# A decoder kernel on one core: attention normalised in channel layout, with its denominators taken from ScalarE's accumulators

## What is computed

```
qh = (q @ Wq + bq).reshape(b, s, H, HD).transpose(0, 2, 1, 3)
kh = (k @ Wk + bk).reshape(b, s, H, HD).transpose(0, 2, 1, 3)
vh = (v @ Wv + bv).reshape(b, s, H, HD).transpose(0, 2, 1, 3)
scores = jnp.einsum('bhqd,bhkd->bhqk', qh, kh) * HD ** (-0.5)
scores = jnp.where(causal, -jnp.inf, scores)
attn = jax.nn.softmax(scores, axis=-1)
out = jnp.einsum('bhqk,bhkd->bhqd', attn, vh)
out = out.transpose(0, 2, 1, 3).reshape(b, s, DIM)
return out @ Wo + bo
```

## Time and profile before

| | |
|---|---|
| median of 3 runs | 371.97 us (371.9 to 372.0) |
| the profiled execution | 369.38 us, its span 367.60 us |
| TensorE matmuls busy | 338.3 us (92% of the span) |
| TensorE weight loads busy | 280.1 us (76%) |
| VectorE busy | 254.6 us (69%) |
| ScalarE busy | 238.9 us (65%) |
| GpSimd busy | 163.5 us (44%) |
| granted TensorE clock | 1.00 throughout |

### The profile page before, as it was taken

How to read it: one execution, slowest core, us unless ns; L and a number is a source line. 1 busy time by engine, 2 the same in 40 slices (tenths; PEclk the granted TensorE clock), 3 DMA queues, 4 the chain that set the end, 5 groups by cost and what they waited for, 6 DMA issues and landing times.

```text
span 367.6 us, 8998 instructions
## 1 busy us (share of the span) xinstructions
PE 338.3 (92%) x3283; PEld 280.1 (76%) x3299; DVE 254.6 (69%) x555; ACT 238.9 (65%) x586; POOL 163.5 (44%) x148
## 2 busy tenths in 40 slices
PE   7878679999999999999999999999999998989697
PEld 3657457987789877987789867987789866858596
DVE  5674786677766976677775976678765966482974
ACT  4552663776756866677847766677848764787551
POOL 4237150364615366363625457362634550445340
PEclk9999999999999999999999999999999999999999
DMA  5940102022031400413023400404014300013300
GB/s 151 307 172 1 31 2 107 37 62 85 1 112 78 144 0 17 171 33 110 0 66 120 143 0 14 169 7 137 0 47 141 116 6 10 30 16 116 116 29 30
DMA packets 22314, 26.97 MB, mean 73 GB/s; under 512 B 2896, under 2 KB 20112, under 8 KB 22288
## 3 DMA queue, kind: packets, MB, share of 16 engines
q1 hardware_dynamic: 21472, 26.52, 22.3%
q10 hardware_dynamic: 816, 0.10, 0.2%
HBM read 24.51 MB, written 2.10 MB: 72 GB/s over the span
## 4 chain that ended last, share of the span: by engine, by line
PE 77%; DVE 9%; issue 7%; ACT 4%; POOL 1%; DMA 1%; ACTq 0%; DVEq 0%; POOLq 0%
PE c L1208 22%; PE a L1208 16%; PE b L1208 14%; PE b1k L1344 7%; PE b1k L1208 6%; PE b2k L1208 4%; DVE negmax L912 2%; PE c L1371 2%; ACT prob L596 1%; ACT probT L558 1%; PE a L1223 1%; DVE scD L893 1%; PE b2k L1223 1%; DMA wk_c<-in_L_attn_Wk 1%; PE a L1301 1%
## 5 line engine op out<-in xcount | busy, mean ns | idle before, releaser
L460 POOL TENSOR_TENSOR w_lo<-w_in,w_hi 128x512 fp32r<-128x512 f32 x32 | 40.8, 1305 | 30.4 <-ACT w_hi L558 26.3
L596 ACT ACTIVATE prob<-b,negmax 128x128 f32<-128x128 f32 x124 | 36.1, 398 | 25.4 <-DVE negmax L912 25.4
L1344 PE MATMUL b1k<-ident,prob 128*128 128x128 f32 x256 | 40.0, 279 | 9.3 <-ACT probT L558 4.5
L466 POOL TENSOR_TENSOR w_lo<-w_in,w_hi 128x512 fp32r<-128x512 f32 x28 | 35.5, 1287 | 28.6 <-ACT w_hi L558 26.8
L453 POOL TENSOR_TENSOR rstA<-varA,minus_half 128x16 f32<-128x16 f32 x8 | 23.4, 2927 | 49.2 <-DVE varA L1047 49.2
L1344 PEld LDWEIGHTS b1k<-ident,prob 128*128 128x128 f32 x256 | 28.1, 140 | 17.3 <-ACT prob L596 7.2
L558 ACT ACTIVATE w_hi<-w_in 128x512 fp32r<-128x512 f32 x64 | 39.1, 653 | 2.6 <-PE b L1208 2.6
L1208 PE MATMUL c<-xTC_hi,w_hi 128*128 128x256 f32 x108 | 31.8, 294 | 0.8 <-DVE xTC_lo L862 0.8
L919 DVE COPY probT<-b1k 128x512 f32<-128x512 f32 x32 | 22.0, 687 | 13.1 <-PE b1k L1344 13.0
L1208 PE MATMUL c<-w_hi,h_hi 128*128 128x256 f32 x96 | 30.8, 321 | 0.1
L1208 PE MATMUL c<-xTC_lo,w_hi 128*128 128x256 f32 x108 | 30.5, 282 | 0.0
(11 more groups left out here) (301 smaller groups left out, 1110.4 us busy)
## 6 DMA issues: line engine op xcount, KB each, us to landing
w_in<-in_L_ffn_w SPq DMA_DIRECT2D x16, 1024.0 KB, 5.6
x_in<-in_x SPq DMA_DIRECT2D x8, 256.0 KB, 2.8
c_in<-in_ctx SPq DMA_DIRECT2D x8, 256.0 KB, 2.9
out<-x2b SPq DMA_DIRECT2D x7, 256.0 KB, 2.2
b_cur<-in_L_ffn_b SPq DMA_DIRECT2D x8, 128.0 KB, 3.0
W_sb<-in_L_attn_W SPq DMA_DIRECT2D x2, 256.0 KB, 4.2
decay_sb<-in_decay SPq DMA_DIRECT2D x1, 512.0 KB, 3.8
h_in<-in_L_xattn_Wk SPq DMA_DIRECT2D x1, 256.0 KB, 4.3
```

The lines of the kernel that those rows point to most:

```text
L460: pool.tensor_tensor(w1_lo[:, :, part], w1_in[:, :, part], w1_hi[:, :, part].bitcast(F32), ALU.subtract).then_inc(s_w1lo, 1)
L466: pool.tensor_tensor(w2_lo[:, part, :], w2_in[:, part, :], w2_hi[:, part, :].bitcast(F32), ALU.subtract).then_inc(s_w2lo, 1)
L596: ins = nc.scalar.activation(prob[:, u % PR, g, :], score_banks[u][:, g * P:(g + 1) * P], ACT.Exp, bias=negmax[:, u, g:g + 1], scale=-1.0)
L1344: ins = nc.tensor.transpose(b1k[:, g * P:(g + 1) * P], prob[:, u % PR, g, :], ident[:, :])
```

## The change

The attention is no longer brought back to tokens to be normalised.

- `exps` gives each ACTIVATE an accumulator output: den[:, u, g] is the row sum of the exponentials, the denominator for each token and head. At blocks 0 and 4 it waits for the reciprocals of the step before (`s_rden`).
- v_pad loses its ones. A head's values stand in the first or the second 16 of its 32 columns, the rest is zero, and `with_values` accumulates two blocks into the same 32 rows. So both sequences fit into one bank (c0, in step 8 a0), and that bank is in channel order of the output as Wo is now loaded: its rows are permuted by eight loads of 16 partitions where there were four of 32 (`WO_LOADS`).
- VectorE's `denominators` takes the reciprocals of den and copies each 16 times side by side (rtok); TensorE's `reciprocals` transposes rtok in four pieces, ScalarE copies them to rdT.
- VectorE's `normalise_attention` multiplies the bank with rdT (attT), ScalarE's `attention_out` rounds it to attT_hi, VectorE's `split_attention` makes attT_lo.
- `pv_out`, `values_to_tokens`, `divide` and `attention_transposes` go. `values` adds the bias in two instructions instead of one, and GpSimd clears all of v_pad at the start.

```diff
-WO_LOADS = 4
+WO_LOADS = 8
...
-        PV_BANK = [c0, b3]
+        PV_BANK = c0
...
-        PV_LAST = [a0, b3]
+        PV_LAST = a0
...
-            for j in range(4):
-                sp.dma_start(xw_in[XG * j:XG * (j + 1), 3, :, :], xWo_v[j % 2, j // 2]).then_inc(s_inO, 16)
+            for j in range(WO_LOADS):
+                sp.dma_start(xw_in[XD * j:XD * (j + 1), 3, :, :], xWo_v[j // 4, j // 2 % 2, j % 2]).then_inc(s_inO, 16)
...
+                    if u % PR == 0 and later(b):
+                        act.wait_ge(s_rden, 2 * b - 1 + u // PR)
                     for g in range(G):
                         ins = nc.scalar.activation(prob[:, u % PR, g, :], score_banks[u][:, g * P:(g + 1) * P],
-                                                   ACT.Exp, bias=negmax[:, u, g:g + 1], scale=-1.0)
+                                                   ACT.Exp, bias=negmax[:, u, g:g + 1], scale=-1.0,
+                                                   accum_out=den[:, u, g:g + 1])
...
-                def pv_out(seq):
-                    act.wait_ge(s_pv, 8 * b + 4 * seq + 4)
...
-                    copy(pvT[:, :], pv_banks[seq][:, :], s_pvT)
...
+                def reciprocals(bank):
+                    act.wait_ge(s_rT, b + 1)
+                    if later(b):
+                        act.wait_ge(s_aT, b)
+                    copy(rdT[:, :, :], bank[:, :].rearrange("p (c t) -> p c t", c=C), s_rdT)
+
+                def attention_out():
                     act.wait_ge(s_aT, b + 1)
-                    copy(attT_hi[:, :, :], bank[:, :].rearrange("p (c t) -> p c t", c=C), s_attT)
+                    if later(b):
+                        act.wait_ge(s_yB, b)
+                    copy(attT_hi[:, :, :], attT[:, :, :], s_attT)
...
+                def denominators(seq):
+
+                    dve.wait_ge(s_prob, 8 * b + PR * (seq + 1))
                     if later(b):
-                        dve.wait_ge(s_aT, b)
-                    kv = k_bank[:, :].rearrange("p (h e) -> p h e", e=VP)
-                    nc.vector.reciprocal(rden[:, seq, :], kv[:, :, XD]).then_inc(s_rden, 1)
+                        dve.wait_ge(s_rT, b)
+                    nc.vector.reciprocal(rden[:, seq, :], den[:, PR * seq:PR * (seq + 1), :]
+                                         .rearrange("p r g -> p (r g)")).then_inc(s_rden, 1)
                     dve.wait_ge(s_rden, 2 * b + seq + 1)
...
+                    nc.vector.tensor_copy(rtok[:, seq, :, :].rearrange("p c (g r e) -> p c g r e", g=G, r=2),
+                                          of_head.unsqueeze(4).broadcast_to([P, C, G, 2, XD])).then_inc(s_rexp, 1)
+
+                def normalise_attention():
+                    dve.wait_ge(s_pv, 8 * (b + 1))
+                    dve.wait_ge(s_rdT, b + 1)
...
+                    nc.vector.tensor_tensor(attT[:, :, :], pv_bank[:, :].rearrange("p (c t) -> p c t", c=C),
+                                            rdT[:, :, :], ALU.mult).then_inc(s_aT, 1)
...
+                def split_attention():
+                    dve.wait_ge(s_attT, b + 1)
+                    nc.vector.tensor_tensor(attT_lo[:, :, :], attT[:, :, :], attT_hi[:, :, :].bitcast(F32),
+                                            ALU.subtract).then_inc(s_attTlo, 1)
...
+                    col = r // 2 * T + bk * P
                     for h in range(G):
                         head = XH // C * (h // 2) + 2 * r + h % 2
-                        ins = mm(bank[VP * h:VP * (h + 1), r * P:(r + 1) * P], v_pad[:, bk, head, :],
-                                 probT[:, u % PR, h, :])
+                        ins = mm(bank[VP * h:VP * (h + 1), col:col + P], v_pad[:, bk, head, :], probT[:, u % PR, h, :],
+                                 start=(r % 2 == 0), stop=(r % 2 == 1))
...
-                def values_to_tokens(seq):
...
-                def attention_transposes(bank):
...
+                def reciprocals(bank):
+                    pe.wait_ge(s_rexp, 2 * (b + 1))
+                    transposes(bank, rtok[:, :, :, :].rearrange("p b c n -> p b (c n)"), s_rT)
```

137 lines of the change are left out of this document (56 added, 81 removed).

## The result

| | before | after |
|---|---|---|
| median of 4 runs | 371.94 us (371.62 to 372.0) | 384.14 us (382.69 to 384.56) |
| the profiled execution | 369.38 us, span 367.6 | 384.56 us, span 382.7 |
| granted TensorE clock, mean of the span | 1.000 | 0.982 |
| a regular step (mean of steps 2 to 6) | 41.76 us | 43.40 us |

The changed kernel is slower by 3.5% (ratio 1.0347, 95% interval 1.0311 to 1.0382). The forecast was 384.7.

The account below looks back on a forecast made before the run. TensorE was taken as the bound on average, with ScalarE setting its pace in two stretches. The terms summed to 208d - 8.15, +12.6 us at d = 0.1, giving 384.7 us against a median of 371.97; range 368 to 400.

Parts of the forecast that it names:

- The price d: ScalarE's extra cost of one accumulating exponential beyond a plain one, taken as 0.1 us, with 256 such exponentials in all.
- the free sums: Rival: the accumulator leaves beside the output, d between 0 and 0.03, total 363.8 (370 at 0.03); chance 0.16.
- the full readout: Rival: each sum costs d = 0.2 like a lone 128x1 instruction, total 405.5; chance 0.18.
- 28 x 0.092 - 0.88: Regular step, forecast as 28d - 0.88 us more each, over five steps 140d - 4.4; here with the measured d.
- 16d: Regular step, first exponentials to second scores: four blocks in ScalarE's gapless piece add +16d.
- 12d - 0.88: Regular step from the second scores on: +4d, then +8d - 0.48, then -0.40 up to the projection.
- -8.15: Whole program: the part of the forecast sum without d, chiefly from removed transposes, copies and waits, in us.
- 208d: Whole program: the readouts that lengthen the run, 208 of 256, each costing d.
- the rival on the other side: The free sums: only the transposes count, so the kernel gets faster, 363.8 us; chance 0.16.
- 24d - 1.3: Step 1: six blocks' readouts count, less 0.47 of ScalarE idle time, 0.44 and 0.40.
- 20d - 0.55: Step 7: readouts add 16d + 4d; fewer transposes and waits, less one more VectorE pair, give -0.55.
- 24d - 1.9: Step 8: readouts add 8d and 16d - 0.5; removed transposes and waits give -0.3 and -1.1.

Follow-up runs that it names:

- e2: The changed kernel without accumulator outputs, den set once to a constant 64 so denominators are not computed; 375.57 us, ratio 1.0120.
- e6: e5 without accumulator outputs, denominators again a constant 64; 367.45 us, ratio 0.9905.
- e1: The kernel before, with only an accumulator output that nobody reads added to every exponential; 387.32 us, ratio 1.0426.
- e5: e3 with VectorE's first rden and rtok pair before block 4's maxima, the second behind block 7's probT copy, readouts kept; 380.50 us.
- e3: The changed kernel with only other instruction orders in steps 7 and 8 (probT copy, qB, Gelu table load, w2 rounding earlier); 379.27 us.

## Why the prediction was right, and where it was not

- **The price d, right.** Taken 0.1, measured 0.092. A block takes 1.51 us from its start to the end of its last readout (83.31 to 84.82), where it was 1.14; 1.5 was said, and under 1.3 would have meant the free sums. The free and the full readout are both excluded by the trace.
- **The regular step, right in size.** With the measured d the working gives 28 x 0.092 - 0.88 = +1.70; it was +1.64. By stretches: 16d = 1.47 against 1.35, the rest 12d - 0.88 = +0.22 against 0.29. The shape of the first was off: I put all of it at the second scores (1.8 us), but TensorE waits earlier too, at the transposes of block 1 for ScalarE (0.53) and of block 2 for VectorE (0.25), and at the scores only 0.69. The wait for attT_lo was 0.27 where 0.3 was said, and the transposes of block 7 wait 0.58, where the matmul timeline of before shows no wait over 0.15 and 0.3 was said.
- **The sum as a sum, wrong.** I added -8.15 for the transposes to 208d and gave the free case 371.97 - 8.2 = 363.8. With d at zero the kernel takes 375.6 (e2), and 367.5 with its orders mended (e6). The step that failed is the sentence on VectorE: "In a regular step both new pairs fit ahead of the probT copy of block 7". They fit behind a late ScalarE. In e2, which has none, they don't: +0.74 a step and not -0.88. With the pairs moved (e6) it is -0.46; why it is not -0.88 is open. The words "has the same shapes but for its sources, and I take 0.7 for it" hide the cause. The sources are what matters: 0.29 for the copy alone, 1.1 to 1.4 beside GpSimd. The forecast did not suffer, since the readouts cover this; the rival on the other side would have.
- **How many readouts count.** 208 of 256 was too many, if e1 is the measure: it gives 15.75 us, 171 of them (e5 and e6 give 13.05, 142 of them). In the regular step it was right (2.40 of 2.58 us); the rest of the excess cannot be placed, because step 1 and the end ran at different clocks in the two traces.
- **Start and step 1, too small.** 24d - 1.3 = +0.9, measured +1.55. The four more loads cost nothing, as said (step 1's first mask matmul stands at 36.78, before at 36.87); two of the periods at half clock lie in step 1.
- **Step 7, too small.** 20d - 0.55 = +1.3, measured +2.7 from its first mask matmul to step 8's (330.24 - 297.65 = 32.59 against 29.87). The wait for probT of block 7 was near (1.74 for 1.9). Not seen: attT_hi stands ahead of qB in ScalarE's queue (0.59), and the clock.
- **Step 8, wrong.** 24d - 1.9 = +0.3 with a gain of 1.1 at the tail, measured +2.6 from step 8's first mask matmul to the end (52.46 against 49.85); the tail lost, with 4.07 us of waiting for the FFN input. I followed the attention's chain there but not the instructions that moved around it: the table load between rdT and attT_hi, and the rounding of w2 that reaches GpSimd late and holds rsC. e3 gives 4.3 us back between step 7 and the end by other orders, a part of it through the clock.
- **The clock, wrong.** "The clock should stay at 1.00" did not hold (see the section on the hardware). At the same mean clock, 0.991, the one run of after that had it took 382.69 us and before 371.53 to 371.86: a difference of 11.0, which is what 208 x 0.092 - 8.15 gives. That it comes out so closely is luck. In the traces the parts that were forecast too small exceed the sum by 4.4 us, and the regular steps fall 0.3 short of it; before alone takes some 3 us more at a mean clock of 0.985 than at 1.000. That fewer readouts on the path and a worse end cancel in the rest is my inference, and no run splits it.

So the forecast was right for its main reason, the readouts on an engine that already set TensorE's pace. It was also helped: d was taken 0.008 too large, 1.7 us in the sum, and the lower clock, which the forecast did not have, cost the changed kernel 1.4 to 1.9 us (its three runs at 0.982 against the one at 0.991).

## What to carry to other kernels

A sum that "comes with" an activation is an instruction of ScalarE, and it costs where ScalarE sets the pace: count it per activation, not per tile. When a change removes work at one bound, ask which other engine then arrives earlier, and beside what; here a copy that was free behind a late ScalarE cost 1 us a step once ScalarE was early. Write down for each rival its own critical path, and don't subtract terms from a sum made for another case.
